# Attention of a four-layer megakernel: the stacked q and k rows are built through DRAM instead of by TensorE, and TensorE's order is written per two steps

## The reference, cut to what matters

```
for l in 0..3:
    q = norm(x) @ Wq + bq ; k = ctx @ Wk + bk ; v = ctx @ Wv + bv     # layer 0: q = norm(x), k = v = ctx
    per batch b (8) and head h (16):  P = softmax(q_h k_h^T / 4)        # 256 x 256 scores; layer 0 adds a mask
    x = x + tanh(gate) * (concat_h(P v_h) @ Wo + bo)                    # layer 0: no Wo
    x = x + tanh(gate) * ffn_l(x)   # 0: light+heavy gelu, 1 and 2: top-2 of 8 experts, 3: ternary weights and a convolution
```

## Time and profile before

| | |
|---|---|
| median of 3 runs | 2010.43 us (2009.65 to 2011.93) |
| the profiled execution's own time | 2009.86 us |
| its span, first to last instruction | 2008.0 us |
| busy share of the span | PE 83%, PE weight loads 59%, DVE 62%, ACT 41%, POOL 19% |
| chain that ended last, by engine | PE 66%, issue 13%, DVE 12%, ACT 3%, POOL 3%, DMA 2% |
| mean granted TensorE clock | 0.914 of full speed |
| bytes moved by DMA | 102.00 MB, mean 51 GB/s |

### The profile page before, as it was taken

How to read it: one execution, slowest core, us unless ns; L and a number is a source line. 1 busy time by engine, 2 the same in 40 slices (tenths; PEclk the granted TensorE clock), 3 DMA queues, 4 the chain that set the end, 5 groups by cost and what they waited for, 6 DMA issues and landing times.

```text
span 2008.0 us, 34955 instructions
## 1 busy us (share of the span) xinstructions
PE 1673.9 (83%) x11187; PEld 1193.7 (59%) x11224; DVE 1238.9 (62%) x2756; ACT 831.4 (41%) x1458; POOL 378.7 (19%) x275
## 2 busy tenths in 40 slices
PE   3999959999998349998996899962799869999685
PEld 2555548856665148887883566631678636665333
DVE  7666763356887615554536587673356567876787
ACT  3555534426664113332321466530344225663332
POOL 2000120000000353345315000006435330002000
PEclk9999969998999669998998799985899987999888
DMA  5004020020000241422112100012342320000000
GB/s 182 23 22 159 0 66 1 1 84 2 1 0 14 74 160 41 143 81 68 37 59 74 37 2 0 0 50 81 127 138 83 94 83 1 1 0 1 0 11 32
DMA packets 66057, 102.00 MB, mean 51 GB/s; under 512 B 6824, under 2 KB 50222, under 8 KB 65840
## 3 DMA queue, kind: packets, MB, share of 16 engines
q1 hardware_dynamic: 52400, 56.76, 8.7%
q0 software_dynamic: 13568, 44.05, 6.8%
HBM read 70.77 MB, written 30.02 MB: 50 GB/s over the span
## 4 chain that ended last, share of the span: by engine, by line
PE 66%; issue 13%; DVE 12%; ACT 3%; POOL 3%; DMA 2%; another core or an unknown queue 1%; DVEq 0%; SPq 0%; POOLq 0%
PE PS L761 6%; PE PS L709 5%; PE PS L736 5%; PE PS L725 4%; PE PS L692 3%; PE PS L941 2%; PE PS L943 2%; PE PS L942 2%; PE PS L919 2%; PE PS L918 2%; PE PS L920 2%; PE PS L643 2%; PE PS L929 2%; PE PS L775 2%; PE PS L803 2%
## 5 line engine op out<-in xcount | busy, mean ns | idle before, releaser
L1606 DVE TENSOR_REDUCE nm<-PS 128x2 f32<-128x512 f32 x512 | 330.1, 687 | 119.8 <-PE PS L709 79.6
L1197 ACT ACTIVATE qk<-PS,cols 128x512 fp32r<-128x512 f32 x256 | 176.4, 689 | 109.8 <-PE PS L695 109.4
L1204 ACT ACTIVATE xng<-PS 128x512 f32<-128x512 f32 x256 | 139.0, 595 | 89.6 <-PE PS L736 51.5
L1204 ACT ACTIVATE probs<-PS 128x512 f32<-128x512 f32 x256 | 139.0, 595 | 88.9 <-PE PS L736 49.8
L490 POOL COPY vbuf<-vall 128x512 f32 (+1 forms) x32 | 19.7, 623 | 646.4 <-PE PS L761 618.8
L1278 ACT ACTIVATE hn<-PS 128x512 f32<-128x512 f32 x117 | 70.1, 600 | 170.7 <-PE PS L920 139.2
L1283 ACT ACTIVATE hh<-PS 128x512 fp32r<-128x512 f32 x117 | 65.9, 596 | 179.0 <-PE PS L929 152.1
L709 PE MATMUL PS<-qk 49*128 49x256 f32 x1024 | 134.3, 342 | 2.4 <-DVE nm L1606 2.4
L941 PE MATMUL PS<-whi,hh 128*128 x468 | 133.5, 285 | 0.0
L942 PE MATMUL PS<-whi,hl 128*128 x468 | 133.4, 285 | 0.0
L943 PE MATMUL PS<-wlo,hh 128*128 x468 | 133.2, 285 | 0.0
(11 more groups left out here) (296 smaller groups left out, 3904.7 us busy)
## 6 DMA issues: line engine op xcount, KB each, us to landing
wslot<-W_dram POOLq DMA_DIRECT2D x16, 1024.0 KB, 9.0
ys_sorted<-yo SPq DMA_DIRECT2D x78, 128.0 KB, 1.7
wide<-ctxT_dram SPq DMA_DIRECT2D x16, 512.0 KB, 5.9
wslot<-W_dram POOLq DMA_DIRECT2D x16, 512.0 KB, 6.0
xg<-xs_sorted SPq DMA_DIRECT2D x62, 128.0 KB, 2.1
xs_sorted<-yo SPq DMA_DIRECT2D x1, 4992.0 KB, 24.1
wproj<-wproj_dram SPq DMA_DIRECT2D x3, 1024.0 KB
wslot<-W_dram SPq DMA_DIRECT2D x2, 1152.0 KB, 9.7
```

The source lines that it names most:

```text
L1197: nc.scalar.activation(qk[:, k % 4, :], PS[:, 0, :], ACT.Identity, bias=col("max_row")).then_inc(sel_done, 1)
L1204: nc.scalar.activation(probs_at(k, h), PS[:, 3 + h, :], ACT.Exp, scale=SCALE).then_inc(exp_done, 1)
L1606: nc.vector.tensor_reduce(nm[:, k % 2, :, at:at + 1], PS[:, 1 + h, :].rearrange("p (q n) -> p q n", q=2), AX.X, ALU.max, negate=True).then ...
```

## The change

The selection by matmuls is gone, with `sel`, the `qk` tiles and the row additions. Instead:

- The four parts of a group of 512 tokens lie in small buffers for two groups (`k_parts`, `q_parts`). SP stores them to a DRAM tensor `parts` in stacked order, three DMAs of 512 KB for k and three for q of each group (`store_k`, `store_q`); the parts of group g can be written only when group g-2 is stored. The columns of the weights are permuted on the host, so that a partition is (d, pair) and the rows fall in place.
- POOL loads the stacked rows of one batch, all 8 pairs, into `stack`, four DMAs of 48 partitions x 8 pairs x 1 KB (393 KB each, 1.57 MB for a batch) with three batches in turn (`load_stack`).
- For each quad one transpose (instead of four) brings the maxima into 8 rows of 128; ACT copies them (`take_rows`), and POOL sends them by DMA to the 49th rows of `stack` (`put_rows`). `mt` has two slots, so `take_rows(n)` waits for the DMA of n-2. `scores_key` comes four quads after `scores_nat` (`KEY`), `times_v` five and `back` six.
- Natural and transposed scores have three PSUM banks each, used in turn by heads. A group of scores waits for the maximum (or exponential) of three groups before.
- PE's order for each turn n: nat(2n), key(2n-8), nat(2n+1), key(2n-7), then the transposes of the maxima of quad n-1 and of the product of quad n-6, then the product of quad n-5.
- The copy of the product moves from DVE to ACT (`take_pv`), the masks from DVE to POOL, and v lies padded in SBUF for all tokens, so that the copies of v by batch are gone (in layer 0 POOL makes four copies of 128x1024 elements).
- On SP's queue `tri` and `iotas` (layer 0) and W1_3, W2_3 (layer 3) now come behind the stores of their layer. The waits of DVE on them stay where they are.

```diff
+            def store_k(l, g):
+                sp.wait_ge(khi_done, GROUPS * l + g + 1)
+                sp.wait_ge(klo_done, GROUPS * l + g + 1)
+                for r, part in enumerate((k_hi(g), k_hi(g), k_lo(g))):
+                    sp.dma_start(rows_of(1, r, g), part.bitcast(F32)).then_inc(k_out[g % 2], 16)
...
+                if l == 0:
+                    for g in range(GROUPS):
+                        store_k(0, g)
+                        store_q(0, g)
+                        if g == 1:
+                            sp.dma_start(v_in, io["ctx"].rearrange("(t p) d -> p t d", p=P)).then_inc(v0_in, 16)
...
                 if l == 0:
                     sp.dma_start(tri[:], io["tri"]).then_inc(later_in, 16)
                     sp.dma_start(iotas[:], io["iotas"]).then_inc(later_in, 16)
...
+            def load_stack(l, b):
+                if b >= SLOTS:
+                    pool.wait_ge(sc_mm, 2 * STEPS * l + 2 * PAIRS * (b - SLOTS + 1))
...
+                for n, out in ((1, k_out), (0, q_out)):
+                    pool.wait_ge(*stored(out, l, b // 2))
+                    for h in range(2):
+                        nc.gpsimd.dma_start(stack[64 * h:64 * h + MAXROW, b % SLOTS, n],
+                                            parts[n, h][:, :, b * S:(b + 1) * S]).then_inc(stack_in[b % SLOTS], 16)
+
+            def put_rows(l, n):
+                j, c, b = QUADS * l + n, 2 * n % PAIRS, 2 * n // PAIRS
+                pool.wait_ge(mt_done, j + 1)
+                nc.gpsimd.dma_start(stack[MAXROW:MAXROW + 65:64, b % SLOTS, 0, c:c + 2, :].rearrange("p c n -> p (c n)"),
+                                    mt[:, j % 2, :]).then_inc(row_in[j % 2], 16)
...
+                load_stack(l, 1)
+                load_stack(l, 2)
+                for n in range(QUADS):
...
+                    put_rows(l, n)
+                    if n % 4 == 3 and n >= 7 and n // 4 + 2 < B:
+                        load_stack(l, n // 4 + 2)
...
+            def attend(l):          # tensor
+                for n in range(QUADS + BACK):
+                    k = n - KEY
+                    for m in range(2):
+                        if n < QUADS:
+                            scores_nat(l, 2 * n + m)
+                        if 0 <= k < QUADS:
+                            scores_key(l, 2 * k + m)
...
+                    if 1 <= n <= QUADS:
+                        max_rows(l, n - 1)
+                    if n >= BACK:
+                        back(l, n - BACK)
+                    if 0 <= n - TIMES_V < QUADS:
+                        times_v(l, n - TIMES_V)
...
+                pe.wait_ge(mt_done, QUADS * l + min(n + TIMES_V, QUADS))      # in times_v
...
+            def attend(l):          # scalar
+                for n in range(QUADS + TIMES_V):
+                    k = n - KEY
+                    if 0 <= k < QUADS:
+                        exps(l, 2 * k)
+                    if 1 <= n <= QUADS:
+                        take_rows(l, n - 1)
+                    if 0 <= k < QUADS:
+                        exps(l, 2 * k + 1)
+                    if n >= TIMES_V:
+                        take_pv(l, n - TIMES_V)
```

More of the change, by code:

```diff
@@ L668, in project @@
                         queries(l, g)
-            def attend(l, i):
-                s0 = STEPS * l + 2 * PAIRS * i
-                j0 = QUADS * l + PAIRS * i
-                peeled = isinstance(i, int)
-                for k in range(2 * PAIRS):
-                    for stage, lag in ((select, 0), (scores_nat, 1), (max_rows, 2), (scores_key, 3), (times_v, 4),
-                                       (back, 5)):
-                        n = k - lag
-                        if n >= 0 or not peeled:
-                            stage(l, s0 + n, n % (2 * PAIRS), 2 * i + n // PAIRS, j0 + n // 2)
@@ L695, in select @@
[L695 to L704 removed]
+                    if l:
+                        pe.wait_ge(v_done, GROUPS * (l + 1))
@@ L705, in scores_nat @@
+                if c == 0:
+                    loads = sum(x % SLOTS == b % SLOTS for x in range(B)) * l + b // SLOTS + 1
+                    pe.wait_ge(stack_in[b % SLOTS], 64 * loads + 16 * (l + 1))
+                if s:
+                    pe.wait_ge(max_done, 2 * s - 1)
+                q, kk = stack[:, b % SLOTS, 0, c], stack[:, b % SLOTS, 1, c]
                 for qt in range(2):
                     for h in range(2):
-                        rows = slice(64 * h, 64 * h + STACK)
-                        mm = pe.matmul(PS[:, 1 + h, qt * S:(qt + 1) * S], qk[rows, k % 4, qt * P:(qt + 1) * P],
-                                       qk[rows, k % 4, 256:512], start=(l > 0 or qt == 0), stop=(l > 0),
-                                       skip_group_check=(l == 0))
+                        rows = slice(64 * h, 64 * h + MAXROW)
+                        mm = pe.matmul(PS[:, (2 * t + h) % 3, qt * S:(qt + 1) * S], q[rows, qt * P:(qt + 1) * P],
+                                       kk[rows], start=(l > 0 or qt == 0), stop=(l > 0), skip_group_check=(l == 0))
@@ L712, in scores_nat @@
                         if l and qt:
                             mm.then_inc(nat_mm, 1)
-                if l == 0:
-                    for h in range(2):
-                        pe.matmul(PS[:, 1 + h, :], bar[:], mask_b[:, (k // PAIRS) % 2, 0], start=False,
-                                  stop=True, skip_group_check=True).then_inc(nat_mm, 1)
-            def max_rows(l, s, k, b, j):
-                pe.wait_ge(max_done, 2 * s + 2)
-                if not (isinstance(s, int) and s == 0):
-                    pe.wait_ge(maxT_done, s)
-                for qt in range(2):
-                    mm = pe.transpose(PS[:, 6, qt * P:(qt + 1) * P], nm[:, k % 2, qt, :], ident[:])
-                mm.then_inc(maxT_mm, 1)
@@ L728, in scores_key, with mask_nat @@
-            def scores_key(l, s, k, b, j):
-                pe.wait_ge(maxT_done, s + 1)
-                if not (isinstance(s, int) and s == 0):
-                    pe.wait_ge(exp_done, 2 * s)
+            def mask_nat(t):
+                if t % PAIRS == 0:
+                    pe.wait_ge(mask_done, t // PAIRS + 1)
+                for h in range(2):
+                    pe.matmul(PS[:, (2 * t + h) % 3, :], bar[:], mask_b[:, t // PAIRS, 0], start=False,
+                              stop=True, skip_group_check=True).then_inc(nat_mm, 1)
@@ new lines, in max_rows, with scores_key @@
+            def max_rows(l, n):
+                j = QUADS * l + n
+                pe.wait_ge(max_done, 4 * j + 4)
+                if j:
+                    pe.wait_ge(mt_done, j)
+                issued = QUADS * l + max(n + 1 - TIMES_V, 0)
+                if issued:
+                    pe.wait_ge(pv_done, issued)
+                pe.transpose(PS[:, 6, S:S + P], nm[:, j % 2, :], ident[:]).then_inc(maxT_mm, 1)
+            def scores_key(l, t):
+                s, b, c = STEPS * l + t, t // PAIRS, t % PAIRS
+                j = s // 2
+                pe.wait_ge(row_in[j % 2], 16 * (j // 2 + 1))
+                if s:
+                    pe.wait_ge(exp_done, 2 * s - 1)
+                q, kk = stack[:, b % SLOTS, 0, c], stack[:, b % SLOTS, 1, c]
```

496 lines of the change are left out of this document (246 added, 250 removed).

## The result

The changed kernel takes 2048.22 us (median; 2045.90 to 2049.18), the kernel before 2011.18 us beside it: a ratio of 1.0178 with a 95% interval of 1.0161 to 1.0195. The forecast was 1943 us in a range of 1893 to 1998. The change makes the kernel 1.8% slower, and the forecast is 105 us too low, on the wrong side of no change.

What follows compares the result with a forecast made beforehand. PE, busy 130 of 130 us in the steady part, was taken to set the time. Terms: -32 x 4 for the attentions, + 28 + 12 + 1 + 15 for starts, + 5 for late loads = -67; 2010.4 - 67 = 1943 us, range 1893 to 1998.

Steps and rivals of the forecast that it cites:

- The turn: Steady attention of layers 1 to 3: one quad takes 3.95 us for 4.99, bounds 3.2 and 4.4.
- layer 0's turn: Layer 0's attention, where the masks stay: one quad takes 5.5 us for 6.68.
- the two that were named: Within a turn: nat(2n+1) waits for DVE's first maximum, until 1.28 us; the product waits for ACT's `take_rows`, until 2.9.
- 1.57 MB lie between 4.0 us ... and 13.5 ...; I take 8, near the pair of 1 MB loads (6.7): Loads of rows within the attention: one batch's load to 48 partitions takes 8 us, so data is in time.
- 5 us over all layers for late ones: Loads within the attention: rows of maxima queued behind a batch's load and landing late cost 5 us in all.
- rival B: Attentions and starts: loads of rows set the turn, late `put_rows` stall `take_rows`; 2042 us at 13.5 us a load; chance 0.13.
- D - 8.3: Rival B's cost of each late load, D being a batch's load time: 19 x (D - 8.3); gain gone at D = 11.8.
- Rival C, the clock: Steady turns: PE idle 0.7 of 3.95 us puts a quarter of turns at 1.2 GHz, 2.6 more each; 1998 us; chance 0.09.
- Layer 0's start: Before layer 0's attention: `tri` behind all stores, 24.8 MB at 391 GB/s, first maximum at about 66; 28 us lost.
- Starts of layers 1 and 2: Before these attentions: layer 1 loses 12 us (6 to the start, 6 for the first `put_rows`), layer 2 loses 1.
- I put 1 us: Layer 2's start: the q groups come further apart there, so only 1 us is lost.
- Layer 3's late weights: Layer 3's start: W1_3 and W2_3 behind q's stores, first maximum at 1674 instead of 1662; 15 us lost.

Runs made afterwards that it cites:

- e17: Changed kernel with 112-partition loads, four maxima slots, late inputs ahead of stores, batch 2's rows later, filler in 128 outermost rows: 1899.49 us, ratio 0.9752.
- e6: Changed kernel with loads of batches 3 to 7 spread over 128 partitions instead of 48, a third of the bytes left out: 1899.17 us, ratio 0.975, one run.
- e3: Changed kernel without the loads of batches 3 to 7 in each layer: 1901.11 us, ratio 0.9758.
- e7: Changed kernel with tri, iotas and layer 3's ternary weights issued ahead of the stores: 1986.46 us, ratio 1.0181.

## Why the prediction was wrong

**The turn: right.** 3.73 to 3.77 us measured in undisturbed turns for 3.95; layer 0's turn is 5.30 us for 5.5 (157.57 - 152.27):

```profile
152.27 1.07 PE L851 MATMUL PS<-probs,vpad 128*32 128x256 f32 x16 [0.23 <-ACT mt L1293]
157.57 1.07 PE L851 MATMUL PS<-xng,vpad 128*32 128x256 f32 x16 [0.23 <-ACT mt L1293]
```

The waits are the two that were named. PE's own order was worth what the forecast said, and e17 collects it: 138 to 139 us per attention.

**The step that failed: "1.57 MB lie between 4.0 us ... and 13.5 ...; I take 8, near the pair of 1 MB loads (6.7)".** A batch takes 10.8 us at 145 GB/s and some 11.5 from its issue. Both anchors go to 128 partitions, and there e6 shows twice the rate. The bound of 13.5 held. The term that rests on it, "5 us over all layers for late ones", measured 81 us. Its rival B, decided at D = 11.8, had the right mechanism, place and sign, with a chance of 0.13, but not the price. It let a late row cost D - 8.3, which is 3.2 at 11.5 us; by its formula that gives 19 x 3.2 = 61 and 2004 us, and the kernel took 2048. In layer 1 the waits are even below the formula (10.4 us over five loads, probably since turns at the lower clock give a row more time), and the larger part, 16.4 us, is the clock, which B had at nothing.

**Rival C, the clock, is not a rival but B's second half.** The forecast asked whether 0.7 us of idle in a turn would lower the clock. It doesn't (1.00 with PE busy 16.6 of 20 us in e3). But a late row stops PE for 1.2 to 4.4 us more, the clock falls to 1.2 GHz, and the turns behind it take 5.5 us, 1.8 more than at full clock where C had 2.6. Loss by wait and loss by clock belong to the same event, and pricing them apart, with a chance for each, left their sum outside the range.

**Layer 0's start: right in kind, 11 us short.** The first maximum came at 76.95 for 66, waiting for `iotas` as named. The step at fault is the rate: 391 GB/s was one full stretch, and from 10 to 77 us the engines move 334 and then 327. The 24.8 MB of the forecast at 330 give 75 us.

**Starts of layers 1 and 2.** The first came 7.9 us later for 6, and its wait for the first row took 8 us at turn 4 for 6. For the second "I put 1 us" failed: +10.8, and PE stood idle for 10.80 us for the first batch's rows. That the groups come further apart says when the last store begins, not how long the first load takes while the stores and the loads of two further batches are under way. The expert weights may have a part in it too. Their four loads of 512 KB are issued at 1125.27 to 1128.67, directly ahead of the first rows (1129.25) in POOL's queue, while in layer 1 they are issued at 412.40, 19 us before the first rows. No run moved them.

**Layer 3's late weights: right.** The sums waited 17.11 us for W, and from the end of layer 2's attention to the first maximum behind the sums it takes 1706.3 - 1321.6 = 384.7 us instead of 1662 - 1292.7 = 369: 15 us, where the forecast's own two times (1674 for 1662) give 12. But as e7 shows, this and layer 0's late `iotas` were not separate terms that could be taken back: another wait of nearly the same length stood right behind each.

What stays open: the split between waiting and the lower clock is counted in layer 1 alone, and no run had late rows at full clock. The price of the stores alone wasn't tried either.

## What to carry to other kernels

When the only transfers in a trace go to 128 partitions, their rate says nothing about one to 48: here it was half, 145 GB/s for about 300, and it was the term on which the sign hung. A small DMA that an engine waits for must not stand behind a large one in a queue with only two slots of slack; here four slots alone gave back 38 us. And where a stall on TensorE's path is likely, price it with the turns at 1.2 GHz that follow, not as the wait alone.

## What the runs showed of the hardware that I had not expected

- A load over 113 partitions came with 15 packets of 4 bytes for each of its 904 pieces of 1 KB (880,896 in all) and took 50 us to land; over 112 partitions, 896 KB in pieces of 1 KB landed in 8 to 9.
- A copy whose pattern has 2 outermost rows used two of 16 engines (share 0.13, 53 GB/s); with 128 outermost rows the same filler went along at the full rate of the start (330 GB/s at a share of 1.04, from 40 to 60 us of e17).
- The type conversion in POOL's queue doubled the packets and took half as much engine time again (32.4% for 22.1% of the engines), yet changed neither the rate of the transfer nor the time of the kernel.
- The same kernel takes 1947 us in some series and 2011 in others, 3% apart; the difference lies in the expert parts, where ACT stands idle. That it is the chip is not shown: chip 9 is on record for the second series (1948.20) and for the third (2010.83). Ratios hold much better (1.0176 against 1.0169 and 1.0181 for kernels that change little), but differences of a few thousandths across the two are not to be read.
